# Attention on TensorE: the matmuls that sum the probabilities are issued head by head in other steps

## The reference

```python
x = x + xattn(_layernorm(x), ctx_2048, ...)        # x: 4 x 512 x 512, context: 4 x 1601 x 512
x = x + ffn(_layernorm(x), ...)                    # 32 experts, top 4, and a shared expert

def xattn(x, context):                             # 16 heads of 32
    ctx_img, ctx_txt = context[:, :257], context[:, 257:]
    q = rms_norm(linear(x, q_w, q_b), norm_q_w)
    k, v = rms_norm(linear(ctx_txt, k_w, k_b), norm_k_w), linear(ctx_txt, v_w, v_b)
    k_img, v_img = rms_norm(linear(ctx_img, k_img_w, k_img_b), norm_k_img_w), linear(ctx_img, v_img_w, v_img_b)
    return linear(attention(q, k, v) + attention(q, k_img, v_img), o_w, o_b)
```

## Time and the profile before

| | us |
|---|---|
| median of 3 runs | 1386.26 |
| lowest and highest | 1382.42 and 1392.75 |
| the profiled execution, its own time | 1390.19 |
| its span, first to last instruction | 1388.3 |
| TensorE busy in it | 1237.4 |
| ScalarE busy in it | 667.9 |
| VectorE busy in it | 889.4 |
| mean granted TensorE clock | 0.964 of full speed |

### The profile page before, as it was taken

The page is one execution under the profiler, slowest core; times in us unless marked ns, Lnnn a source line. Parts: engine busy times, 40 slices in busy tenths (PEclk is TensorE's granted clock), DMA queues, the critical chain, the costliest instruction groups (busy, mean ns, idle before and its releaser), DMA issues. The chain is left out here.

```text
span 1388.3 us, 22059 instructions
## 1 busy us (share of the span) xinstructions
PE 1237.4 (89%) x8916; PEld 460.8 (33%) x8916; DVE 889.4 (64%) x1169; ACT 667.9 (48%) x910; POOL 184.3 (13%) x299
## 2 busy tenths in 40 slices
PE   4988999999999899989989998995778998988986
PEld 2542222444222245422224442221433333333332
DVE  5765877777587878757688776886666653222221
ACT  4546886345788534578853448883211011111111
POOL 0210000132000013200001320000210001333332
PEclk9999999999999999999999999997979999999999
DMA  7200000221000112200011122010800102899884
GB/s 276 84 25 15 2 2 7 85 69 69 24 1 1 51 41 69 92 1 1 2 64 36 61 76 92 1 62 25 337 8 31 39 0 82 279 289 311 288 283 110
DMA packets 38388, 117.80 MB, mean 85 GB/s; under 512 B 6544, under 2 KB 6800, under 8 KB 33040
## 3 DMA queue, kind: packets, MB, share of 16 engines
q1 hardware_dynamic: 33168, 105.60, 21.5%
q0 software_dynamic: 5120, 10.82, 3.7%
HBM read 95.67 MB, written 20.73 MB: 84 GB/s over the span
## 5 line engine op out<-in xcount | busy, mean ns | idle before, releaser
L566 ACT ACTIVATE work<-ps 128x1024 f32<-128x1024 f32 (+1 forms) x416 | 403.1, 1021 | 61.0 <-PE ps L1039 58.7
L1046 PE MATMUL ps<-work,vals 128*32 128x512 f32 (+2 forms) x1792 | 236.6, 604 | 0.9 <-ACT work L566 0.8
L862 PE MATMUL ps<-wts,work 128*128 128x512 f16 x864 | 205.3, 389 | 14.6 <-DVE work L595 14.6
L1039 PE MATMUL ps<-quer,keys 32*128 32x512 f16 x2496 | 171.8, 377 | 25.1 <-ACT work L566 9.3
L778 DVE TENSOR_TENSOR work<-work 128x2048 f32<-128x2048 f32 x64 | 146.6, 2291 | 11.4 <-ACT work L566 7.3
L778 DVE TENSOR_TENSOR attn<-attn,work 128x2048 f32<-128x2048 f32 x64 | 146.6, 2290 | 10.8 <-ACT work L566 7.3
L862 PE MATMUL ps<-wts,hl 128*128 128x512 f16 x480 | 116.1, 395 | 23.2 <-DVE hl L595 23.2
L862 PEld LDWEIGHTS ps<-wts,work 128*128 128x128 f16 x864 | 83.7, 100 | 116.6 <-issue 16.9
L1039 PEld LDWEIGHTS ps<-quer,keys 32*128 32x128 f16 x2496 | 46.2, 92 | 214.5 <-ACT work L566 189.2
L1786 PE MATMUL f_ps<-wring,xgt 128*80 128x512 f32 x256 | 117.1, 601 | 0.0
L1372 ACT ACTIVATE yf<-f_ps,wc 80x512 f32<-80x512 f32 x32 | 21.9, 683 | 171.3 <-PE f_ps L1801 143.3
(11 more groups left out here) (208 smaller groups left out, 1445.7 us busy)
## 6 DMA issues: line engine op xcount, KB each, us to landing
wring<-in_wx SPq DMA_DIRECT2D x32, 1536.0 KB, 7.9
raw<-in_ctx SPq DMA_DIRECT2D x52, 256.0 KB, 2.8
work<-in_x SPq DMA_DIRECT2D x4, 1024.0 KB, 5.5
table<-nums SPq DMA_DIRECT2D x16, 256.0 KB, 2.3
out<-x1s SPq DMA_DIRECT2D x16, 256.0 KB, 2.3
work<-in_x SPq DMA_DIRECT2D x12, 256.0 KB, 4.9
x<-work SPq DMA_DIRECT2D x12, 256.0 KB, 2.0
x2t_rows<-nums SPq DMA_DIRECT2D x12, 256.0 KB, 2.5
```

The costliest lines, as they stand in the source:

```text
L566: act.activation(prob[0:rows, s % PROBS, 2 * half:2 * half + 2, :], ps[0:rows, 2 * pair:2 * pair + 2, :], ACT.Exp, scale=SCALE).then_inc(a ...
L862: mm = pe.matmul(out, lhs(a, c)[:, cols], wts[:, w, z, c * D:(c + 1) * D], start=(k == 0), stop=(k == len(steps) - 1))
L1039: mm = pe.matmul(ps[:, 2 * pair + h % 2, :], k[h * HD:(h + 1) * HD, :], q[h * HD:(h + 1) * HD, :], start=(e == 0), stop=(e == len(terms) - 1))
L1046: mm = pe.matmul(ps[h * HD:(h + 1) * HD, NUM, :], vals[a:z, ORDER[n], g * P + h * HD:g * P + (h + 1) * HD], prob[a:z, s % PROBS, h, :], st ...
```

## The change

Only TensorE's program in `attention` is changed. The arithmetic is the same, apart from the order in which the parts of a denominator are added.
- The four denominator matmuls of n = 0 are split: heads 0 to 2 stay, head 3 goes ahead of the wait of step n = 1. Of those of n = 1, heads 0 and 1 stay, and 2 and 3 go ahead of the wait of n = 2.
- In n = 2 the denominator of the mixed tile (four matmuls of 128 rows) is cut in a text half (rows 0 to 63) and an image half (rows 64 to 127). The image numerator of a head (rows 64 to 127, bank NUM) is followed by the text half of the denominator (rows 0 to 63, bank DEN) of the same head: `numerator`, `mixed_part`, for each of four heads.
- The text numerator of the mixed tile, which stood first in n = 3, is paired with the image half of the denominator (`mixed_text`): heads 0 and 1 at the end of n = 3, heads 2 and 3 at the start of n = 4.
- The counts on `a_av` for n = 2 and n = 3 are given by the two `mixed_text` in n = 4.
- The text denominators of the group before come as one matmul of 512 columns in each of n = 6, 7, 8 and 9 (head 0, 1, 2, 3), where they were four matmuls of 256 columns in n = 6 and four in n = 8.

```diff
+                def image_part(s, h, rows, first=False):
+                    return pe.matmul(ps[h * HD:(h + 1) * HD, DEN, :], ones[0:rows, 1, s // KT, :],
+                                     prob[0:rows, s % PROBS, h, :], start=first, stop=False)
+
+                def mixed_part(s, h, a, z):
+                    return pe.matmul(ps[h * HD:(h + 1) * HD, DEN, :], ones[a:z, 2, s // KT, :],
+                                     prob[a:z, s % PROBS, h, :], start=False, stop=False)
+
+                def text_part(g, h, last=False):
+                    return pe.matmul(ps[h * HD:(h + 1) * HD, DEN, :], ones[:, 0, g, :], sums[g % 2][:, h, :],
+                                     start=False, stop=last)
+
+                def mixed_text(s, h):
+                    numerator(s, h, 0, SPLIT, False, False)
+                    return mixed_part(s, h, SPLIT, P)
 
                 def weighted(s):
                     g, n = s // KT, s % KT
+                    if n == 1:
+                        image_part(s - 1, 3, P, first=(g == 0)).then_inc(a_av, 1)
+                    if n == 2:
+                        image_part(s - 1, 2, LAST)
+                        image_part(s - 1, 3, LAST).then_inc(a_av, 1)
+                    if n == 4:
+                        mixed_text(s - 2, 2).then_inc(a_av, 1)
+                        mixed_text(s - 2, 3).then_inc(a_av, 1)
                     pe.wait_ge(a_exp, unit(bb, 2 * s + 1))
...
-                        numerator(s, 0, P, True, False)
-                        denominator(g, 1, prob[:, s % PROBS, :, :], P, first=(g == 0)).then_inc(a_av, 1)
+                        numerators(s, P, True, False)
+                        for h in range(3):
+                            image_part(s, h, P, first=(g == 0))
                     elif n == 1:
-                        numerator(s, 0, LAST, False, False)
-                        denominator(g, 1, prob[:, s % PROBS, :, :], LAST).then_inc(a_av, 1)
+                        numerators(s, LAST, False, False)
+                        image_part(s, 0, LAST)
+                        image_part(s, 1, LAST)
                     elif n == 2:
-                        numerator(s, SPLIT, P, False, True).then_inc(a_img, 1)
-                        denominator(g, 2, prob[:, s % PROBS, :, :], P).then_inc(a_av, 1)
+                        for h in range(4):
+                            mm = numerator(s, h, SPLIT, P, False, True)
+                            mixed_part(s, h, 0, SPLIT)
+                        mm.then_inc(a_img, 1)
                     elif n == 3:
                         pe.wait_ge(a_ni, gn(bb, g))
-                        numerator(s - 1, 0, SPLIT, True, False)
-                        numerator(s, 0, P, False, False).then_inc(a_av, 1)
+                        numerators(s, P, True, False)
+                        mixed_text(s - 1, 0)
+                        mixed_text(s - 1, 1)
                     else:
-                        numerator(s, 0, P, False, n == KT - 1).then_inc(a_av, 1)
-                        if g > 0 and n in (6, 8):
+                        numerators(s, P, False, n == KT - 1).then_inc(a_av, 1)
+                        if g > 0 and 6 <= n < 10:
                             if n == 6:
                                 pe.wait_ge(a_sum, added(bb, g - 1, ADDS - 1))
-                            at = 0 if n == 6 else L // 2
-                            mm = denominator(g - 1, 0, sums[(g - 1) % 2], P, at, at + L // 2)
-                            if n == 8:
+                            mm = text_part(g - 1, n - 6)
+                            if n == 9:
                                 mm.then_inc(a_den, 1)
```

More of the change, by code:

```diff
@@ L1041, in scores, with numerator, numerators @@
                     mm.then_inc(a_sc, 1)
-                def numerator(s, a, z, first, last):
+                def numerator(s, h, a, z, first, last):
                     g, n = s // KT, s % KT
+                    return pe.matmul(ps[h * HD:(h + 1) * HD, NUM, :],
+                                     vals[a:z, ORDER[n], g * P + h * HD:g * P + (h + 1) * HD],
+                                     prob[a:z, s % PROBS, h, :], start=first, stop=last)
+                def numerators(s, rows, first, last):
@@ L1045, in numerator @@
                     for h in range(4):
-                        mm = pe.matmul(ps[h * HD:(h + 1) * HD, NUM, :],
-                                       vals[a:z, ORDER[n], g * P + h * HD:g * P + (h + 1) * HD],
-                                       prob[a:z, s % PROBS, h, :], start=first, stop=last)
-                    return mm
[L1051 to L1055, removed]
+                        mm = numerator(s, h, 0, rows, first, last)
@@ L1098, in attention @@
                 pe.wait_ge(a_sum, added(bb, NG - 1, ADDS - 1))
-                denominator(NG - 1, 0, sums[(NG - 1) % 2], P, last=True).then_inc(a_den, 1)
+                for h in range(4):
+                    mm = text_part(NG - 1, h, last=True)
+                mm.then_inc(a_den, 1)
             def one_pass(p):
```

## The result

The changed kernel takes 1432.17 us in the median of four runs (1426.73 to 1437.58), against 1387.72 us for the kernel before (1382.42 to 1392.75): 1.032 of it, with a 95% interval of 1.028 to 1.035. The forecast was 1431. The profiled execution spans 1427.8 us, 39.5 more than before.

The account below looks back on a forecast made before the run. Plain attention steps were taken as paced by ScalarE, heavy ones by TensorE. 16 x 1.19 + 12 x 2.18 = 45.2, less 0.7, gave + 44.5 on 1390.2: 1434.7, less 3.9 for the median: 1431 us, range 1410 to 1446.

Parts of the forecast that it names:

- A step costs the larger of ScalarE's 1.96 and TensorE's work in it: Attention steps: ScalarE paces plain ones at 1.96 us, TensorE heavy ones; a group adds up to 28.90 us, 28.88 measured.
- Passes, not matmuls: Attention's fp32 matmuls of 512 columns: 0.87 us a pass, however few heads; rival of a quarter price, 1372 us, chance 0.05.
- The text part: n = 6 to 9, groups 1 to 3: a lone text matmul makes each step 2.62 us, + 2.18 a group.
- n = 0 to 2 keep their passes: First three steps of a group: two passes each, as before; only n = 2 grows, by about 0.03 us.
- the row halves pair: Pairs in n = 2, 3 and 4: both row halves run in one pass; rival of unpaired halves, 1473 us, chance 0.06.
- n = 3: Fourth step of a group: two passes as before, plus TensorE's wait for DVE's image numerator copy, 0.12, 0.14 with rounding.
- n = 4: Fifth step of a group: an extra pass and a new wait for n = 2's probability buffer, 2.98 us, 1.02 over 1.96.
- The give-back at the last batch's end: Last batch: DVE's last add ends 2.7 us later while the group's steps grow by 3.4, so 0.7 is given back.
- The sum: All four attention stretches: 16 x 1.19 + 12 x 2.18 = 45.2 us, less 0.7 given back, + 44.5 us.
- longer text steps: n = 6 to 9 at 2.75 us each would be 6 us more in all, 1437.

Follow-up runs that it names:

- the series of one, two and four heads: Kernel before with text denominators of 512 columns for one, two or four heads a step from n = 6: 1410.14 us (1.018), 1389.28, 1384.20.
- `pairs_and_heads`: Kernel before with the mixed tile's halves paired in n = 2 and 3, and image denominators given out by heads over n = 0 to 2: 1388.36 us.
- `changed_late_count`: Changed kernel with heads 2 and 3 of `mixed_text` at the end of n = 3, n = 2's buffer count on n = 4's first numerator: 1429.3 us.

## Why the prediction was right, point by point

- **A step costs the larger of ScalarE's 1.96 and TensorE's work in it.** Held in every kernel run: no step was faster than 1.95, and the steps of 2.19, 2.6 and 2.76 are TensorE's passes added up; that of 2.35 is 0.06 over its sum of 2.29. The steps that are longer than either are n = 3 and n = 4, where one engine waits for another.
- **Passes, not matmuls.** Shown by the series of one, two and four heads (2.59, 2.60, 2.62). It was the point on which the sign hung, and the trace of before could only bound it, by a lone fp16 matmul and a whole-array fp32 one. The text part is 2.1 of the 3.5 us that a group other than the first grew by (forecast 2.18), and costs 1.8% by itself.
- **n = 0 to 2 keep their passes, and the row halves pair.** Right, to 0.02 us. The forecast did not say what `pairs_and_heads` shows: that the pairing had a pass to give, which the handing-out took.
- **n = 3.** The mechanism was right, the term too small: 0.12 to 0.14 forecast, 0.25 measured (2.99 for 2.74). From the pairs' start at 190.02 to the copy's start it was 1.18 (1.14 forecast), and from the copy's end at 191.89 to the numerators at 192.04 0.15, where I had taken 0.04.

```profile
191.20 0.69 DVE L764 COPY nums<-ps 128x512 f32<-128x512 f32 x1 [5.32 <-PE ps L1045]
```

- **n = 4.** The new wait was right (2.98 forecast, 3.05 measured), and `changed_late_count` shows it by itself. The activation starts 1.97 us after the scores at 194.03, 0.07 later than I summed.

```profile
196.00 3.90 ACT L566 ACTIVATE work<-ps 128x1024 f32<-128x1024 f32 x4 [2.14 <-PE ps L1059]
```

- **The give-back at the last batch's end.** TensorE waits 3.08 us for DVE's last add, for 3.84 before: 0.76, for a forecast of 0.7.

```profile
995.87 1.87 PE L1063 MATMUL ps<-attn,ones 128*32 128x512 f32 x8 [3.08 <-DVE attn L778]
```

- **The sum.** Attention grew by 47.5 us in the profile, of which 1.5 is the step at lower clock; forecast 44.5. The other 1.5 of excess is in the steps: 16 x 0.18 for n = 3 and n = 4, less 12 x 0.07 for n = 6 to 9 and 16 x 0.03 for n = 1 and 2. The runs' medians differ by 44.5. That this equals the forecast to the tenth is luck, as the profiled run's 39.5 shows: the clock, of which the sum says nothing, moves the rest by several us. The upper end of the range, 1446, was not worked out beyond the 1437 of longer text steps and a spread of 6 us.

## What to carry to other kernels

When small matmuls run side by side on parts of the array, count passes, that is the most loaded part, and not matmuls: a pass with one head in it lasts as long as one with four. To spread such work thinly over steps that have a little slack, cut the moving columns for all parts at once, and leave no part out. And when a reader of a buffer or a bank is moved to a later step, look at what is released by it. One count that came a step later cost 1.0 us, more than the pass it belonged to (0.8 in n = 2). And if another engine copies a result while the next matmuls wait for that copy, put other work between them: half a pass behind the pairs hid the wait.

## What the runs showed of the hardware

- Eight fp32 matmuls of 64 rows by 32 columns, on two row halves and four column parts, start within 0.05 us and take as long as four of 128 rows: 1.09 us to the last end, for 1.07.
- Short fp32 matmuls cost what their columns say. From the start of four to that of the scores it is 0.33 us with 128 columns (169.34 to 169.67), 0.55 with 256 (194.85 to 195.40 in the earlier trace rows) and 0.98 with 512 (165.28 to 166.26): 0.22 for each 128 columns, and 0.11 besides.
- TensorE starts what stands behind a matmul that has to wait for its part of the array. In the trace of before, two sets of five one-column fp16 matmuls, each on columns 0, 32, 64, 96 and 0, follow each other. Windows that end at 1093.5 and 1093.7 us show eight of them started, and then nine:

```profile
1093.23 0.60 PE L1715 MATMUL f_ps<-oneh,tok 128*1 128x512 f16 x8
1093.23 0.81 PE L1715 MATMUL f_ps<-oneh,tok 128*1 128x512 f16 x9
```

  The fifth starts at 1093.44, and the sixth needs the same columns, which a matmul keeps for 0.21 us. So the three others that have started by 1093.5 are the seventh to the ninth, ahead of the sixth.
- The stretch at the lower clock level behind a 4 us pause of TensorE differs, within a run and from run to run: 4.06 to 5.30 us for the same twelve matmuls. Over the three projections of the two profiled executions that was 6.3 us.
